# Down products of the routed tiles: from plain fp32 to three products of weights and m split in two

## What is computed

```python
xf = layernorm(x)                                  # 2048 tokens x 512
scores = softmax(xf @ gate_w.T)                    # 8 experts
weights, idx = top_k(scores, 2)
h = einsum('td,eid->eti', xf, w1)                  # every expert: 512 -> 256
g = silu(h) * einsum('td,eid->eti', xf, w3)
eo = einsum('eti,edi->etd', g, w2)                 # 256 -> 512, the "down" product
comb = einsum('tke,tk->te', one_hot(idx), weights)
y = einsum('etd,te->td', eo, comb)
z = silu(xf @ ws1.T) * (xf @ ws3.T) @ ws2.T        # one shared expert
x = x + y + z
```

## Time and profile before

| | |
|---|---|
| three timed runs, median | 1418.67 us (1416.2 to 1424.42) |
| the profiled execution | 1417.02 us, of it 1415.3 us in the span of the profile |
| mean granted TensorE clock | 0.992 |
| PE busy, share of the span | 96% (its weight loads 77%) |
| DVE, ACT, POOL busy | 55%, 45%, 37% |
| routed part | about 1192 us to the end |

### The profile page before, as it was taken

The page is one execution under the profiler, slowest core; times in us unless marked ns, Lnnn a source line. Parts: engine busy times, 40 slices in busy tenths (PEclk is TensorE's granted clock), DMA queues, the critical chain, the costliest instruction groups (busy, mean ns, idle before and its releaser), DMA issues.

```text
span 1415.3 us, 24170 instructions
## 1 busy us (share of the span) xinstructions
PE 1360.5 (96%) x8372; PEld 1088.1 (77%) x8372; DVE 783.5 (55%) x2037; ACT 629.9 (45%) x1182; POOL 516.7 (37%) x485
## 2 busy tenths in 40 slices
PE   8999999999999999999999999999988999999994
PEld 6888888888888888888887778777766887776662
DVE  5787765333333333333466666665676586666662
ACT  4444441111111111111138777777787233777772
POOL 4554542202020202021336554445435112565662
PEclk9999999999999999999999999999999999999997
DMA  6000011001010101010100000000011834465553
GB/s 253 1 0 0 0 66 69 6 40 45 1 45 1 44 0 44 0 45 0 49 27 21 2 20 20 20 20 3 6 46 44 328 120 153 83 109 97 105 98 45
DMA packets 20535, 73.43 MB, mean 52 GB/s; under 512 B 2320, under 2 KB 3344, under 8 KB 18000
## 3 DMA queue, kind: packets, MB, share of 16 engines
q0 software_dynamic: 10176, 25.17, 9.1%
q1 hardware_dynamic: 10256, 46.93, 9.1%
HBM read 52.95 MB, written 19.14 MB: 51 GB/s over the span
## 4 chain that ended last, share of the span: by engine, by line
PE 84%; DVE 6%; ACT 3%; issue 2%; DMA 2%; POOL 1%; DVEq 0%; POOLq 0%; ACTq 0%
PE ps L768 21%; PE ps L770 20%; PE ps L769 20%; PE ps L1016 5%; PE ps L1218 5%; PE ps L1008 2%; PE ps L1040 2%; DVE den L1665 2%; DMA h_rows<-hd 1%; PE ps L1125 1%; ACT cols L1448 1%; ACT cols L1436 1%; PE ps L1188 1%; PE ps L1034 1%; PE ps L1054 1%
## 5 line engine op out<-in xcount | busy, mean ns | idle before, releaser
L768 PE MATMUL ps<-feat,wsplit 128*128 128x512 f32 (+1 forms) x672 | 247.2, 368 | 3.2 <-PE ps L770 2.1
L770 PE MATMUL ps<-feat,wsplit 128*128 128x512 f32 (+1 forms) x672 | 244.5, 364 | 0.0
L769 PE MATMUL ps<-feat,wsplit 128*128 128x512 f32 (+1 forms) x672 | 244.3, 364 | 0.0
L1300 ACT ACTIVATE sg<-ps 128x512 f32<-128x512 f32 x64 | 38.3, 598 | 369.6 <-PE ps L770 369.6
L1585 DVE TENSOR_TENSOR m_f<-ps,sg 128x512 f32<-128x512 f32 x64 | 44.2, 691 | 245.8 <-ACT sg L1300 245.8
L1850 DVE CUSTOM_DVE_ANT_0 cols<-ps,msk 128x256 f32<-128x256 f32 (+1 forms) x512 | 148.9, 353 | 54.1 <-PE ps L1008 33.7
L527 POOL CAST wsplit<-wraw 128x3072 fp32r<-128x3072 f32 x9 | 24.8, 2752 | 399.4 <-PEq L956 387.1
L768 PEld LDWEIGHTS ps<-feat,wsplit 128*128 128x128 f32 x672 | 126.6, 188 | 26.3 <-issue 6.6
L1436 ACT COPY cols<-ps 128x512 f32<-128x512 f32 x192 | 112.1, 585 | 76.7 <-PE ps L1016 76.6
L770 PEld LDWEIGHTS ps<-feat,wsplit 128*128 128x128 f32 x672 | 126.6, 188 | 20.1
L769 PEld LDWEIGHTS ps<-feat,wsplit 128*128 128x128 f32 x672 | 126.7, 188 | 19.7
(11 more groups left out here) (285 smaller groups left out, 3051.7 us busy)
## 6 DMA issues: line engine op xcount, KB each, us to landing
wraw<-weights SPq DMA_DIRECT2D x11, 1536.0 KB, 6.4
rawx<-weights SPq DMA_DIRECT2D x8, 1536.0 KB, 13.3
ctx_raw<-ctx_t SPq DMA_DIRECT2D x8, 512.0 KB, 4.6
h_rows<-hd POOLq DMA_DIRECT2D x16, 256.0 KB, 4.2
out<-acc SPq DMA_DIRECT2D x4, 1024.0 KB, 5.2
qkv_raw<-weights SPq DMA_DIRECT2D x6, 512.0 KB, 7.3
acc<-x SPq DMA_DIRECT2D x1, 3072.0 KB, 17.8
acc<-x SPq DMA_DIRECT2D x2, 512.0 KB, 6.9
```

The costliest lines, as they stand in the source:

```text
L768: nc.tensor.matmul(out_, w_hi, m_hi, start=first, stop=False)
L769: nc.tensor.matmul(out_, w_lo, m_hi, start=False, stop=False)
L770: return nc.tensor.matmul(out_, w_hi, m_lo, start=False, stop=last)
```

## The change

The routed tiles' down products go through `three`, as their up products do. ACT casts the expert's down weights (128x1024) for each routed tile (`dx_hi`), DVE subtracts (`dx_lo`), into `down_even` (over four tiles of `acc` that have been stored by then) and `down_odd` (over the shared expert's down weights). m transposed is split for all tiles (`mT_hi` to fp32r, then `mT_lo` on DVE), and `mT_x` goes. PE no longer reads the expert's number and no longer waits for the raw weights. The wait for the first store, `x_stored[0]`, moves from `mT_hi` to `scale_rows`. `dx_hi(i+1)` and `dx_lo(i+1)` stand ahead of `ux_hi(i+2, 1)` and `ux_lo(i+2, 1)` in their engines' lists. The diff without the table of semaphore names (`mT_x` goes, `dx_hi` and `dx` come):

```diff
@@ -300,7 +300,9 @@
         up_even = at("up_even", [P, 2, UPN], F32R, off=split_at + 8 * SLOT + 2 * 4096)
         up_odd = wsplit[:, 0, :, 0:UPN]
         hg = at("hg", [P, HG, D], F32, off=acc_at + 8 * 4 * D)
-        mT_x = at("mT_x", [P, 2, JB, P], F32, off=acc_at + 3 * 4 * D)
+
+        down_even = at("down_even", [P, 2, JB * D], F32R, off=acc_at + 4 * 4 * D)
+        down_odd = wsplit[:, 0, :, UPN:UPN + JB * D]
         yx = at("yx", [P, 3, D], F32, off=acc_at + 0 * 4 * D)
 
         region(temp_at)
...
@@ -1180,10 +1182,7 @@
 
             def m_t(g):
                 pe.wait_ge(d["m"], g + 1)
-                if g <= TILES:
-                    after(pe, d["mT"], g)
-                else:
-                    pe.wait_ge(d["mT_x"], g - TILES)
+                after(pe, d["mT"], g)
                 for j in range(JB):
                     tr = nc.tensor.transpose(ps[:, 6, g % 2 * GROUP + j * P:g % 2 * GROUP + (j + 1) * P], m_x[:, g % 2, j * P:(j + 1) * P], ident[:, :])
                 tr.then_inc(d["mT_ps"], 1)
...
@@ -1203,19 +1202,18 @@
                     if j < len(also):
                         logits(also[j], range(KB))
 
-            def raw_of(g):
-                e = pe.value_load(expert_of[0:1, g - TILES:g - TILES + 1], min_val=0, max_val=EXPERTS - 1)
-                return rawx[:, bass.ds(e, 1), :].rearrange("p o n -> p (o n)")
-
-            def down_x(g, raw):
-                pe.wait_ge(d["mT_x"], g - TILES + 1)
+            def down_x(g):
+                s = g - TILES
+                pe.wait_ge(d["mT"], g + 1)
                 if g - 2 >= TILES:
                     pe.wait_ge(d["y"], g - 1 - TILES)
                 else:
                     pe.wait_ge(d["acc"], g - 1)
+                pe.wait_ge(d["dx"], s + 1)
+                w = down_odd if s % 2 else down_even
                 for j in range(JB):
-                    o = UPN + j * D
-                    mm = nc.tensor.matmul(ps[:, 4 + g % 2, :], mT_x[:, g % 2, j, :], raw[:, o:o + D], start=(j == 0), stop=(j == JB - 1))
+                    o = slice(j * D, (j + 1) * D)
+                    mm = three(pe, ps[:, 4 + g % 2, :], mT[:, g % 2, 0, j, :], mT[:, g % 2, 1, j, :], w[:, 0, o], w[:, 1, o], j == 0, j == JB - 1)
                 mm.then_inc(d["down"], 1)
 
...
@@ -1252,7 +1250,6 @@
                 summed_piece(name, BATCH)
             head_t(4)
             head_t(5)
-            raw = {}
             for i in range(ALL):
                 m_t(i)
                 if i == 0:
...
@@ -1271,15 +1268,10 @@
                     running_counts()
                 if i > TILES - 2 and i + 2 < ALL:
                     head_t(i + 2)
-                if i + 1 == TILES:
-                    pe.wait_ge(d["experts"], 1)
-                    for e in range(EXPERTS):
-                        pe.wait_ge(raw_expert[e], 16)
                 if i + 1 < TILES:
                     up_d(i + 1, LOGITS_IN_UP.get(i, ()))
                 elif i + 1 < ALL:
                     up_x(i + 1)
-                    raw[i + 1] = raw_of(i + 1)
                 for g in HEADS_BEHIND.get(i, ()):
                     head_t(g)
                 if i == 12:
...
@@ -1289,7 +1281,7 @@
                 if i < TILES:
                     down_d(i, LOGITS_IN_DOWN.get(i, ()))
                 else:
-                    down_x(i, raw[i])
+                    down_x(i)
 
 
         def mlp_act(act, s_):
...
@@ -1501,12 +1493,7 @@
                 act.wait_ge(d["mT_ps"], g + 1)
                 after(act, d["down"], g - 1)
                 m_in = ps[:, 6, g % 2 * GROUP:(g % 2 + 1) * GROUP].rearrange("p (j n) -> p j n", j=JB)
-                if g < TILES:
-                    nc.scalar.copy(mT[:, g % 2, 0, :, :], m_in).then_inc(d["mT_hi"], 1)
-                else:
-                    if g == TILES:
-                        act.wait_ge(x_stored[0], 16)
-                    nc.scalar.copy(mT_x[:, g % 2, :, :], m_in).then_inc(d["mT_x"], 1)
+                nc.scalar.copy(mT[:, g % 2, 0, :, :], m_in).then_inc(d["mT_hi"], 1)
 
             raw = {}
 
...
@@ -1524,8 +1511,18 @@
                 w = up_odd if s % 2 else up_even
                 nc.scalar.copy(w[:, 0, o], rawx[:, bass.ds(raw[g], 1), o].rearrange("p o n -> p (o n)")).then_inc(d["ux_hi"], 1)
 
+            def dx_hi(g):
+                s = g - TILES
+                act.wait_ge(d["down"], g - 1)
+                if s == 0:
+                    act.wait_ge(x_stored[1], 16)
+                w = down_odd if s % 2 else down_even
+                nc.scalar.copy(w[:, 0, :], rawx[:, bass.ds(raw[g], 1), UPN:UPN + JB * D].rearrange("p o n -> p (o n)")).then_inc(d["dx_hi"], 1)
+
             def scale_rows(g):
                 s = g - TILES
+                if s == 0:
+                    act.wait_ge(x_stored[0], 16)
                 act.wait_ge(d["down"], g + 1)
                 if s >= 3:
                     act.wait_ge(added[(s + 1) % 2], 16 * ((s - 1) // 2))
...
@@ -1574,6 +1571,8 @@
                     ux_hi(TILES, 1)
                 if i == TILES - 2:
                     hT_hi_d(i + 2)
+                if i > TILES - 2 and i + 1 < ALL:
+                    dx_hi(i + 1)
                 if i > TILES - 2 and i + 2 < ALL:
                     ux_hi(i + 2, 1)
             scale_rows(ALL - 1)
...
@@ -2052,6 +2051,13 @@
                 w = up_odd if s % 2 else up_even
                 nc.vector.tensor_tensor(w[:, 1, o], rawx[:, bass.ds(raw[g], 1), o].rearrange("p o n -> p (o n)"), w[:, 0, o], ALU.subtract).then_inc(d["ux"], 1)
 
+            def dx_lo(g):
+                s = g - TILES
+                dve.wait_ge(d["dx_hi"], s + 1)
+                w = down_odd if s % 2 else down_even
+                nc.vector.tensor_tensor(w[:, 1, :], rawx[:, bass.ds(raw[g], 1), UPN:UPN + JB * D].rearrange("p o n -> p (o n)"), w[:, 0, :],
+                                        ALU.subtract).then_inc(d["dx"], 1)
+
             def hx_lo(g):
                 dve.wait_ge(d["hx_hi"], g - TILES + 1)
                 nc.vector.tensor_tensor(hT_x[:, g % 2, 1, :, :], ps[:, 2 + g % 2, :].rearrange("p (k n) -> p k n", k=KB), hT_x[:, g % 2, 0, :, :],
...
@@ -2074,8 +2080,7 @@
             for i in range(ALL):
                 if i == 6:
                     router_probs(1)
-                if i < TILES:
-                    mT_lo(i)
+                mT_lo(i)
                 if i == 0:
                     mult_d(1)
                     dve.wait_ge(c["oT_hi"], 1)
...
@@ -2140,6 +2145,8 @@
                     nc.vector.tensor_tensor(acc[:, i, :], ps[:, 4 + i % 2, :], acc[:, i, :], ALU.add).then_inc(d["acc"], 1)
                 if i == TILES - 2:
                     hx_lo(i + 2)
+                if i > TILES - 2 and i + 1 < ALL:
+                    dx_lo(i + 1)
                 if i > TILES - 2 and i + 2 < ALL:
                     ux_lo(i + 2, 1)
 
```

More of the change, by code:

```diff
@@ L393, in decoder_layer @@
             mT_ps="m transposed in PSUM", mT_hi="its hi", mT="its lo too", down="sums in PSUM", acc="shared sums added to the residual",
-            y="routed sums scaled", hx_hi="routed tiles of h transposed, their hi", hT_x="their lo too", ux_hi="halves of a tile's up weights with hi", ux="split", others="whether a tile follows one of another expert", mT_x="routed tiles' m transposed in SBUF",
+            y="routed sums scaled", hx_hi="routed tiles of h transposed, their hi", hT_x="their lo too", ux_hi="halves of a tile's up weights with hi", ux="split", others="whether a tile follows one of another expert", dx_hi="routed tiles' down weights with hi", dx="split",
             pool="GpSimd's own small steps", dve="the vector engine's")
```

## The result

The changed kernel takes 1436.72 us in the median of four runs (1432.32 to 1439.08), the kernel before 1420.24 us, measured again beside it: a ratio of 1.0107 with a 95% interval of 1.0078 to 1.0136. It is slower, by 16.5 us between these medians; the forecast was 1433.5 us, in a range of 1417 to 1446. The profiled execution took 1432.32 us, where 1431.8 was forecast, 1430.6 of them in the span; before it was 1417.02 and 1415.3.

A forecast was written before the change was run, and what follows sets the result against it. PE was taken to bound the kernel before, and the late half 1 the changed one, at 5.55 us a tile: 1417.0 + 14.8 = 1431.8 us profiled, plus 1.65 to the median of runs, 1433.5 us, range 1417 to 1446.

The forecast's parts named there:

- What bounds it: Routed part of the kernel before: PE sets the pace, busy 59.98 of 60.00 us, 5.13 us a tile.
- PE's own work: Routed down product on PE: 1.36 us instead of 1.72, so PE's work falls from 5.13 to 4.77 us a tile.
- The late half: Half 1 of the up weights: ready 3.84 us after silu, PE asks at 3.21, stopping over 0.6 us a tile.
- PE's restart: From half 1 ready to PE's start: 0.05 us taken; the other price, 0.36, would add 11.5 us.
- The second loop: Over half 0 of the up weights: m at 6.21 us after silu, transposes 6.68, PE free at 6.71; it fits.
- Entry and tail: First routed period 6.06 us; PE's removed entry waits worth at most 0.36 us, once; the tail moves as a whole.
- full gain: Routed part: PE stays the bound despite the late half, 14.0 us less than before, 1404.7 us; chance 0.08.
- Level: Half 1 is in time and the loop over half 0 decides, 5.15 us a tile, 1418.2 us; chance 0.12.
- POOL's queue: POOL's adds, held over both DVE subtractions in a row, set the pace at 6.26 us, 1459 us; chance 0.06.
- The granted clock: TensorE's clock falls from 2.4 to 1.2 GHz as PE stops each tile, 162 us more, 1581 us; chance 0.02.

The follow-up runs named there:

- the plain product: Changed kernel with all new splits kept, but PE makes the down product in plain fp32 from raw weights and unsplit m: 5.58 us a tile.
- half 1 first: Changed kernel with half 1 of the up weights ahead of the down weights on ACT and DVE: 1421.39 us, 0.9994 against before, 5.13 us a tile.

## Why the prediction was right, point by point

- *What bounds it*: PE, in the routed part. Shown by the kernel before with the read moved: with nothing late, 5.128 us a tile, PE's own 5.13. After the change it is half 1's subtraction: a period of 5.57 us where PE's own work is 4.77 by the forecast, which no kernel tried here got down to.
- *PE's own work*: 1.36 us for the down product. Measured 1.36. That it is worth nothing here was measured with the plain product.
- *The late half*: ready 3.84 us after silu; measured 3.83. Its terms: silu to cast 0.28, measured 0.29; cast to subtraction 1.18, measured 1.18; subtraction to the next 1.15, measured 1.14; the last one 1.23, measured 1.22. Where I had to choose between 1.15 and 1.36 for two subtractions in a row, the lower end holds.
- *PE's restart*: 0.05 or 0.36. Measured 0.05 (half 1 ready at 1283.46, PE at 1283.51). From there to silu 1.66 was forecast, 1.69 is measured (1283.51 to 1285.20). This is the 0.02 us by which the period of 5.57 exceeds 5.55, and over 36 tiles it makes most of the 0.7 us by which the stretch was underrated.
- *The second loop*, over half 0: forecast at 6.21 us for m, "with nothing to spare". Measured 5.99 (silu 1279.63, m 1285.62), and even that is set by the new silu 0.42 us ahead of it: half 0's subtraction had started at 1284.36, so m could have come at 5.88. The term that was too large is from the copy of m to half 0's cast: 0.74 us when nothing holds the cast of h between them (1281.80 to 1282.54), not 1.07. It didn't matter in the changed kernel; with half 1 first, m came to be the bound.
- *Entry and tail*: the first period 6.06, measured 6.08; tile 16's silu 0.54 us sooner, where I had said at most 0.36; the tail 0.36 longer, where I had said unchanged. Tile 16's silu came anywhere from 1195.4 to 1198.4 us in eight profiled executions, so the 0.54 us measure no term. The tail was 28.11 and 28.13 us in the two executions that have the down product of before in its order, and 28.47 and 28.77 in the two that have the changed one, so some of it is real; nothing here explains it. That the two nearly cancel is luck.
- *Rivals*: full gain falls, PE waits in each tile. Level is not what this order does. Half 1 first measured 5.13 us where level had 5.15, but that is luck: with 0.74 us in place of 1.07 the same loop gives 4.98, and nine periods over 5.25 us make up the rest. POOL's queue falls: the adds average 1606 ns between 1200 and 1400 us where they took 2030 between 1200 and 1390 before. The granted clock was 1.00 between 1200 and 1400 us, with PE busy 91%.

The chain that ended last, in order of time (start, us), shows one turn of the loop as the forecast has it, silu to silu:

```profile
1274.07 0.05 ACT sgx L1490
...
1274.35 1.05 ACT down_even L1520
...
1275.53 0.90 DVE down_even L2058
1276.43 0.25 issue
1276.67 1.23 DVE wsplit L2052
1277.94 0.50 PE ps L770
...
1279.63 0.05 ACT sgx L1490
```

The 0.90 and 0.25 are together the 1.14 from one subtraction's start to the next.

## What to carry to other kernels

Work that is moved from a full engine to ones with slack costs by where it stands in their lists, not by how much it is: put it behind everything that the full engine will ask for sooner. Work out, for each hand-over in a steady loop, when it is ready and when it is asked for, both from the same event; the smallest difference is what an insertion ahead of it may take, here 0.88 us, of which the shorter down product itself took 0.36, against a chain grown by 1.15. Shortening what comes before it makes the full engine ask sooner. And in these kernels the register read behind a wait was paid once that spot was on the loop; ahead of the wait it was hidden.

## What the runs showed of the hardware that I had not expected

- The register read on DVE is bare for about 0.6 us when it stands behind the wait, and now and then longer. Half 0's subtraction starts 1.81 to 1.83 us after its cast starts in most tiles of the kernel before, of which 1.05 are the cast; with the read ahead of the wait, and nothing else changed, 1.19 to 1.20. Where DVE gets there late, the idle time without a releaser was 0.20 us in some periods and 0.33, 0.74, 1.22 and up to 1.88 in others. What makes it last longer at times isn't known from these runs.
- With more subtractions of two SBUF operands POOL's adds were shorter: 2030 ns on average before, 1606 in the changed kernel. What counts is which starts first. In the kernel before, the add of 2.63 us at 1332.09 began 0.06 us behind the start of such a subtraction (1332.03), and all adds of 2.4 us and more began 0.06 to 0.30 us behind one; adds that began up to 0.05 us ahead of one took 1.59 or 1.60, as do those of the changed kernel's loop, some 0.9 us ahead of one (1280.21 and 1281.10 in the tile shown). So it is a matter of phase, not of how many there are. The Trainium skill's page "SBUF — State Buffer", section "Who interferes with whom", has DVE instructions with two SBUF inputs contend with GpSimd ones that read SBUF; the long adds fit it, and the short ones show that the number of such instructions by itself predicts nothing.
- The granted clock can dip in a stretch ahead of the part under study. In the shared tiles, with PE busy 28.62 of 30 us, the changed kernel with only the read moved shows

```profile
1120.00:1150.00 30.00, 28.62 (x162) 25.39 (x161) 13.83 (x51) 8.50 (x15) 2.71 (x5) 0.83 0.78 313
```

  and the changed kernel itself

```profile
1120.00:1150.00 30.00, 28.72 (x176) 24.74 (x175) 18.70 (x95) 11.49 (x19) 2.22 (x5) 1.00 0.70 273
```

  A mean of 0.83 is 2.4 GHz with about a third of the stretch at 1.2 GHz. It had been at 1.00 between 1100 and 1120 us, with PE busy 19.90 of 20 us and the loads of the experts' weights running (0.98 to 1.02 of the transfer engines from 1110 us on), and it falls to 0.50 behind a stop of PE ahead of the router's matmuls (1.38 us, until 1128.12). That stop alone doesn't explain it: all twelve profiled executions have it, with 0.89 to 1.41 us, and the one with 1.41 keeps 1.00. Four of them have this dip, 0.77 to 0.83, and the same four had 0.83 between 1070 and 1080 us; their silu of tile 16 is at 1202.6 to 1205.2 us, in the other eight at 1195.4 to 1198.4. It isn't a property of an edit: those kernels are alike up to there. The timed runs of the changed kernel fit it, with 1432.32 us at a mean granted clock of 0.993 and 1439.08 at 0.988. This is why the routed stretch, and not the whole time, carries the verdicts on the kernels that were timed once.
